# A count taken from the one-hots, a running sum moved behind the places, and three idle products in place of eight

## The chip, the cores and the metric

The kernel runs on one core of a Trainium2 chip. The metric is the device time of one execution in microseconds (us); lower is better. Engines are named as in the profile: PE is TensorE (PEld its weight loads), DVE is VectorE, ACT is ScalarE, POOL is GpSimd, SP is SyncE, whose queue issues the plain DMAs.

## The reference, cut to what matters

Two blocks act on 2048 rows of 128 numbers. The first has a causal attention with decay and, beside it, four layers of a mixture of 16 experts with one router each; a row goes to the one expert with the highest logit:

```python
def _unipool_layer(xt, router, W1, W2):
    probs = jax.nn.softmax(xt @ router, axis=-1)
    w, idx = jnp.max(probs, axis=-1), jnp.argmax(probs, axis=-1)
    def body(acc, params):
        w1, w2, i = params
        h = jax.nn.silu(xt @ w1) @ w2          # 128 -> 512 -> 128
        return acc + jnp.where(idx == i, w, 0.0)[:, None] * h, None
    ...
xt, _ = jax.lax.scan(step, xt, routers)        # L = 4 layers, E = 16 experts
```

The second block (a gated recurrence and a smaller mixture of experts) follows and is not touched.

## The kernel before

**Layers and tiles.** Each of the four layers works on rows sorted by expert, in 31 tiles of 128 rows (16 full tiles' worth of rows and 15 that padding may need). In `tile_mm` PE multiplies a tile by its expert's first matrix (L2258, 8 matmul records of a tile) and the tile before it by the second one (L2273, 8 records). The second product also gives the logits of the next layer's router. ACT scales and stores the result in `xrow` (L1722, `y_ev`).

**The next layer's order.** While a layer runs, its tiles' rows are placed for the next layer in six groups: tiles 0 to 7, 8 to 15, 16 to 19, 20 to 23, 24 to 27 and 28 to 30. For a group, DVE does four things. `choose` makes the one-hots `hot` (L1117 to L1125, `hot_ready`). `sum_hot` adds them up over the group's tiles and adds the sum so far (L1026, L1029, `hot_summed`). `weigh` makes the routing weight and copies the row's old place (L1138 to L1141). `rooms` and `place` turn counts and ranks into a row number for each row (L1002 to L1010, L1195 to L1202, `pos_ready`), and `carry_on` keeps what the next group needs (L1016 to L1020). Between `choose` and `rooms`, PE's `ranks` makes each row's rank within its expert and, at L2130, the count of each expert so far: one product of ones with `hot_sum[g]`. POOL scatters each tile's rows to memory by an indirect DMA (L734), one after the other, once the group's places are there.

**A helper.** `step(x)` makes DVE wait until x has ended; `mark(x)` only counts it. On DVE an instruction behind a `mark` may start before the marked one has ended.

**The end of a layer.** Groups 4 and 5 come behind the last tiles, and this stretch comes three times (ahead of layers 1, 2 and 3):

```python
choose(l, NGR - 2)
sum_hot(l, NGR - 2)
weigh(l, NGR - 2)
rooms(l, NGR - 2)
place(l, NGR - 2)
choose(l, NGR - 1)
weighted_scores(PHASE[l][0])
last_rooms(l)
```

PE does `ranks` of group 4 behind tile 30's place in the loop, then the last tiles' products, two products of attention scores (L2201), `last_ranks` (from L2141 on; it waits for `hot_ready`, `hot_summed` and `carried`), and a share of the attention (`retrieve` L2211, `scores` L2201), whose products alternate with DVE's weighting (L1217, L1219). Then it does eight products of the identity with itself into a corner of a bank that nobody reads (L2332; the profile records each as two matmuls):

```python
for n in range(WARM if l < L - 1 else 0):
    pe.matmul(PS[:, 1, 512 - P:512], ident[:, :], ident[:, :], start=True, stop=True)
```

**The start of the next layer.** SP waits until every scattered tile has landed (L610), then loads tile 0 and tile 1 (L587, one DMA each), the tags, and the other tiles in pairs (L596). PE waits for each of the first two tiles and transposes it (L2249); DVE copies three experts' matrices to a ring (L1259), then copies the two transposed tiles out (L1265); then PE begins the products of tile 0 (L2258).

Of the kernel before, what the change touches and what calls it, by code (L numbers as in the profile page):

```python
# [14 lines left out]
def build(nc, ins, out):  # L15
    x_in = ins["L0_attn_x"]
    B, S, D = x_in.shape
# [11 lines left out]
    NG = NT // G  # L29
# [9 lines left out]
    GROUPS = ((0, 8), (8, 16), (16, 20), (20, 24), (24, 28), (28, NS))  # L39
# [11 lines left out]
    WB = 4  # L51
    WARM = 8
    AHEAD = 2
# [99 lines left out]
    with ExitStack() as ctx:  # L153
# [788 lines left out]
        def _(dve):  # L942
            seq = [0]

            def step(ins_):
                seq[0] += 1
                ins_.then_inc(dve_seq, 1)
                dve.wait_ge(dve_seq, seq[0])
# [178 lines left out]
            def sum_hot(l, g):  # L1127

                tt = group_slots(g)
                dve.wait_ge(hot_ready, NG + l * NGR + g + 1)  # L1130
                dve.wait_ge(hot_summed, NG - 1 + l * (NGR - 1) + g)
                sum_so_far(g, hot[:, tt, :])

            def weigh(l, g):

                i, tt = NG + l * NGR + g, group_slots(g)
                dve.wait_ge(exp_done, i + 1)
                step(dve.tensor_scalar(ex[:, tt, :], ex[:, tt, :], -1.0, 1.0, ALU.mult, ALU.add))  # L1138
                step(dve.reciprocal(ex[:, tt, :], ex[:, tt, :]))
                mark(dve.tensor_reduce(xrow[:, tt, D + 1], ex[:, tt, :], AX_X, ALU.add))  # L1140
                step(dve.tensor_copy(xrow[:, tt, D], tags[:, GROUPS[g][0]:GROUPS[g][1], 0]))  # L1141

# [39 lines left out]
            def place(l, g):  # L1182
# [11 lines left out]
                else:  # L1194
# [7 lines left out]
                dve.tensor_tensor(pos[:, GROUPS[g][0]:GROUPS[g][1]], posf[:, tt], trash[:, GROUPS[g][0]:GROUPS[g][1]],  # L1202
                                  ALU.add).then_inc(pos_ready, 1)
                o = carry_on(g)
                if g == NGR - 2:
# [86 lines left out]
            for l in range(L):  # L1292
# [23 lines left out]
                if l < L - 1:  # L1316
                    choose(l, NGR - 2)
                    sum_hot(l, NGR - 2)
                    weigh(l, NGR - 2)
# [749 lines left out]
        def _(pe):  # L2069
# [39 lines left out]
            def ranks(l, g):  # L2109
# [4 lines left out]
                pe.wait_ge(hot_ready, i + 1)  # L2114
                if g < NGR - 1:
                    pe.wait_ge(hot_summed, NG - 1 + l * (NGR - 1) + g + 1)
                if g >= 2:
# [7 lines left out]
                for t in range(n - 1):  # L2125
                    later = o[:, (t + 1) * E:].rearrange("p (t e) -> p t e", e=E)
                    pe.matmul(later, ones_bf[:, :], hot[:, s0 + t:s0 + t + 1, :].to_broadcast([P, n - 1 - t, E]),
                              start=False, stop=(t == n - 2))
                if g < NGR - 1:
                    m = pe.matmul(o_count, ones_bf[:, :], hot_sum[:, g, :], start=True, stop=True)  # L2130
                m.then_inc(rank_mm, 1)

# [528 lines left out]
```

## Time and profile before

| | |
|---|---|
| median of 3 runs | 668.79 us (667.09 to 668.97) |
| the profiled execution, its own time | 668.92 us |
| its span, from the first to the last instruction | 667.1 us |
| mean granted clock of PE | 0.939 |
| PE busy | 578.5 us, 87% |
| DVE busy | 480.8 us, 72% |
| ACT busy | 433.2 us, 65% |
| POOL busy | 385.2 us, 58% |

The profile records one execution. Busy times are shares of the span; 1.8 us of the profiled execution's time lie outside the span. The granted clock is that of PE as a share of 2.4 GHz. In the views below a number before a name is the start in us from the span's start.

### The profile page before, as it was taken

How to read it: one execution, taken by the hardware profiler on the slowest of the kernel's cores; microseconds unless marked ns; L12 is line 12 of the kernel's file. 1: busy time of each engine (PE TensorE's matmuls, PEld its weight loads, DVE VectorE, ACT ScalarE, POOL GpSimd, SP SyncE). 2: the span in 40 equal slices, each digit the busy share in tenths (PEclk: the TensorE clock that was granted, in tenths of full speed). 3: DMA queues.
4: the chain of work that ended last, by engine and by line, in shares of the span. 5: the costliest groups of instructions: out<-in, count | busy, mean ns of one | idle time of the engine just before them, and what ended most of it. 6: DMA issues, size and time to landing. Idle time of an engine off the chain costs nothing.

```text
span 667.1 us, 14440 instructions
## 1 busy us (share of the span) xinstructions
PE 578.5 (87%) x4659; PEld 492.3 (74%) x4659; DVE 480.8 (72%) x1407; ACT 433.2 (65%) x1016; POOL 385.2 (58%) x433
## 2 busy tenths in 40 slices
PE   1969899999999999979999598977867877798896
PEld 1759899959997799959999346955645664576785
DVE  7543456874588556875321789889999999997946
ACT  4374366754677356735677578978877887887533
POOL 7372005740357104752546311786999999998974
PEclk9979899999999999979999888869888788989999
DMA  7953264226521373115331200000000000000002
GB/s 250 344 183 39 59 175 78 60 52 143 101 59 50 56 169 73 53 51 66 73 63 44 64 1 1 2 1 1 1 1 0 0 1 2 0 1 1 2 2 64
DMA packets 109690, 39.86 MB, mean 60 GB/s; under 512 B 86098, under 2 KB 103538, under 8 KB 109490
## 3 DMA queue, kind: packets, MB, share of 16 engines
q1 hardware_dynamic: 105138, 29.64, 20.1%
q0 software_dynamic: 4480, 9.30, 4.1%
q8 instruction: 40, 0.66, 0.4%
q14 instruction: 32, 0.26, 0.1%
HBM read 20.32 MB, written 18.59 MB: 58 GB/s over the span
## 4 chain that ended last, share of the span: by engine, by line
PE 56%; DVE 29%; ACT 7%; POOL 5%; issue 3%; DVEq 0%; POOLq 0%
PE PS L2273 17%; PE PS L2258 16%; PE PS L2211 3%; ACT W1s L1897 2%; PE PS L2177 2%; DVE W1s L1521 2%; DVE W1s L1490 2%; DVE W2s L1376 2%; PE PS L2440 2%; DVE PS L1492 2%; DVE PS L1494 2%; DVE PS L1514 2%; DVE PS L1496 2%; PE PS L2201 2%; PE PS L2456 2%
## 5 line engine op out<-in xcount | busy, mean ns | idle before, releaser
L734 POOL DMA_INDIRECT sorted_x<-xrow,pos x93 | 90.5, 973 | 148.6 <-ACT xrow L1722 77.8
L2273 PE MATMUL PS<-W2s,hbuf 128*128 x992 | 140.1, 285 | 0.0
L2258 PE MATMUL PS<-hbuf,swt 128*128 128x128 f32 x992 | 132.6, 278 | 2.9 <-DVE hbuf L1265 2.9
L2273 PEld LDWEIGHTS PS<-W2s,hbuf 128*128 128x128 f32 x992 | 127.7, 192 | 0.4
L2258 PEld LDWEIGHTS PS<-hbuf,swt 128*128 128x128 f32 x992 | 121.7, 193 | 3.7 <-DVE swt L1259 2.0
L1714 ACT ACTIVATE hbuf<-PS 128x512 f32<-128x512 f32 x124 | 73.1, 590 | 51.9 <-PE PS L2258 49.5
L1722 ACT ACTIVATE xrow<-PS,tags 128x144 f32<-128x144 f32 (+1 forms) x124 | 46.8, 377 | 42.3 <-PE PS L2273 40.3
L1897 ACT ACTIVATE W1s<-W1s,ab 128x128 f32<-128x128 f32 x168 | 51.3, 391 | 16.4 <-DVE W1s L1524 16.3
L2440 PE MATMUL PS<-ewT,xT 128*128 128x512 f32 x64 | 38.6, 735 | 21.5 <-ACT W2s L1948 21.4
L850 POOL TENSOR_TENSOR W1s<-W1s,kT 128x1024 f32<-128x1024 f32 x22 | 52.3, 2383 | 7.0 <-DVE W1s L1524 5.8
L1259 DVE COPY swt<-W1s 128x512 f32 x64 | 27.1, 427 | 38.5 <-PE PS L2258 34.5
L739 POOL DMA_INDIRECT results<-xrow,pos x31 | 31.1, 1004 | 37.8 <-ACT xrow L1722 25.8
L1268 DVE STREAM_TRANSPOSE hbuf<-hbuf 128x128 f32<-128x128 f32 x116 | 33.3, 300 | 18.0 <-DMA hbuf<-sorted_x 16.8
L2456 PEld LDWEIGHTS PS<-W2s,ident 128*128 128x128 f32 x256 | 35.4, 215 | 11.8 <-issue 11.8
L1765 ACT ACTIVATE swt<-W1s 128x512 f32 x60 | 37.8, 631 | 3.2 <-issue 1.1
L2492 PE MATMUL PS<-ident,W1s 128*128 128x128 f32 x256 | 34.7, 280 | 5.6 <-POOL W1s L850 5.6
L1948 ACT ACTIVATE W2s<-PS,selbuf 128x128 f32<-128x128 f32 x128 | 35.1, 368 | 4.3 <-issue 4.0
L2440 PEld LDWEIGHTS PS<-ewT,xT 128*128 128x128 f32 x64 | 13.0, 226 | 33.0 <-ACT W2s L1948 23.1
L2456 PE MATMUL PS<-W2s,ident 128*128 128x128 f32 x256 | 35.2, 297 | 1.7 <-DVE xres L1438 1.7
L2492 PEld LDWEIGHTS PS<-ident,W1s 128*128 128x128 f32 x256 | 29.5, 144 | 7.2 <-POOL W1s L850 6.5
L1897 ACT ACTIVATE W1s<-xrow,ab 128x128 f32<-128x128 f32 x88 | 26.9, 397 | 8.5 <-DVE xrow L1524 8.5
L1219 DVE SCALAR_TENSOR_TENSOR wdec<-PS,wdec 128x512 f32<-128x512 f32 (+3 forms) x24 | 13.4, 556 | 22.1 <-PE PS L2201 21.4
(420 smaller groups left out, 1356.2 us busy)
## 6 DMA issues: line engine op xcount, KB each, us to landing
hbuf<-sorted_x SPq DMA_DIRECT2D x224, 32.0 KB
sorted_x<-slotbuf SPq DMA_DIRECT2D x9, 520.0 KB, 3.7
W2s<-in_L_ffn_W_dram SPq DMA_DIRECT2D x16, 256.0 KB, 5.0
W1s<-in_L_ffn_W_dram SPq DMA_DIRECT2D x1, 4096.0 KB, 16.8
sorted_x<-slotbuf SPq DMA_DIRECT2D x1, 2015.0 KB, 7.9
sorted_x<-xrow,pos POOLq DMA_INDIRECT x109, 2.4
sorted_x<-slotbuf SPq DMA_DIRECT2D x3, 455.0 KB, 2.9
xres<-in_L_attn_x_dram SPq DMA_DIRECT2D x4, 256.0 KB, 3.6
```

What stands on the lines that cost most here:

```text
L734: pool.indirect_dma_start(xs_dram[l + 1][:, :], bass.IndirectOffsetOnAxis(ap=pos[:, t:t + 1], axis=0), xrow[:, t % NR, 0:XW], None).then_i ...
L850: pool.tensor_tensor(qX[t % QR], X[(t + 1) % NX], Qc[:, t, :, :].unsqueeze(1).to_broadcast([P, 2 * HD, HP, HD]), ALU.mult).then_inc(r_read ...
L1714: act.activation(hTs[:, (c - 1) % 2, :], PS[:, 2 + (c - 1) % 2, :], ACT.Silu).then_inc(h_act, 1)
L1722: act.activation(xrow[:, t % NR, 0:w], PS[:, 4 + c % 2, 0:w], ACT.Copy, scale=tags[:, t, 1:2]).then_inc(y_ev, 1)
L1765: act.activation(w1st[:, c % WB, :], W1s[:, bass.ds(w, FF)], ACT.Copy).then_inc(w1_act, 1)
L1897: o = act.activation(aX[:, :, h, :], X[t % NX][:, :, h, :], ACT.Copy, scale=ab[:, t, h:h + 1])
L1948: o = act.activation(scaled[:, t % 2, e, :], PS[:, 4 + e // 4, e % 4 * D:(e % 4 + 1) * D], ACT.Copy, scale=sel[:, t, e:e + 1])
L2258: m = pe.matmul(PS[:, 2 + n, f * P:(f + 1) * P], w1st[:, (c - 1) % WB, f * P:(f + 1) * P], xring[:, (c - 1) % R, :], start=True, stop=True)
L2273: m = pe.matmul(PS[:, 4 + n, 0:w], hTs[:, n, f * P:(f + 1) * P], W2s[:, f * YW:f * YW + (E - 1) * NF + w][:, bass.ds(w2, w)], start=(f == ...
L2440: m = pe.matmul(PS[:, 4 + n, :], xT[:, t * P:(t + 1) * P], ewT[:, n * 512:(n + 1) * 512], start=True, stop=True)
L2456: pe.matmul(o, ident[:, :], scaled[:, t % 2, e, :], start=(e == 0), stop=False)
L2492: m = pe.matmul(o, qXw[t % QR][:, i, :], ident[:, :], is_transpose=True, start=(i == 0), stop=(i == HD - 1))
```

## The change

Three edits. (1) For group 4 the count no longer comes from `hot_sum[4]`: PE multiplies ones by `hot_sum[3]` and by each of the four tiles' one-hots and adds the five in the bank, so `ranks` of group 4 waits for the one-hots and for the sum of group 3; `sum_hot` of group 4 moves from ahead of `weigh` into `place`, behind the write of the places and ahead of `carry_on`. (2) In `weigh`, for all five groups that use it, the copy at L1141 is marked and not waited for. (3) `WARM` goes from 8 to 3.

```diff
-    WARM = 8
+    WARM = 3
...
                 mark(dve.tensor_reduce(xrow[:, tt, D + 1], ex[:, tt, :], AX_X, ALU.add))
-                step(dve.tensor_copy(xrow[:, tt, D], tags[:, GROUPS[g][0]:GROUPS[g][1], 0]))
+                mark(dve.tensor_copy(xrow[:, tt, D], tags[:, GROUPS[g][0]:GROUPS[g][1], 0]))
...
                                   ALU.add).then_inc(pos_ready, 1)
+                if g == NGR - 2:
+                    sum_hot(l, g)
                 o = carry_on(g)
...
                     choose(l, NGR - 2)
-                    sum_hot(l, NGR - 2)
                     weigh(l, NGR - 2)
...
-                if g < NGR - 1:
-                    pe.wait_ge(hot_summed, NG - 1 + l * (NGR - 1) + g + 1)
+                pe.wait_ge(hot_summed, NG - 1 + l * (NGR - 1) + (g + 1 if g < NGR - 2 else g))
...
-                if g < NGR - 1:
+                if g < NGR - 2:
                     m = pe.matmul(o_count, ones_bf[:, :], hot_sum[:, g, :], start=True, stop=True)
+                else:
+                    pe.matmul(o_count, ones_bf[:, :], hot_sum[:, g - 1, :], start=True, stop=False)
+                    for t in range(n):
+                        m = pe.matmul(o_count, ones_bf[:, :], hot[:, s0 + t, :], start=False, stop=(t == n - 1))
                 m.then_inc(rank_mm, 1)
```

## Rows read from the trace of the kernel before

**Rows 1.** Busy us (x instructions) of PE, PEld, DVE, ACT, POOL in layer 1, PEclk, DMA

```profile
150.00:200.00 50.00, 50.00 (x444) 49.81 (x444) 31.24 (x123) 31.96 (x66) 14.86 (x16) 1.00 0.48 100
```

**Rows 2.** Chain that ended last, group 4 ahead of layer 1: start, us, what

```profile
131.03 0.23 DVE hot L1125
...
131.29 0.27 DVE hot_sum L1026
...
131.59 0.17 DVE hot_sum L1029
131.75 0.35 DVE ex L1138
...
132.85 0.17 DVE xrow L1141
...
133.04 0.19 DVE room L1002
...
135.46 0.16 DVE pos L1202
135.63 0.10 DVE shift L1016
```

**Rows 3.** The same chain, from the attention's products to the transposes of layer 1

```profile
145.28 1.98 PE PS L2211 x4
147.26 1.78 PE PS L2332 x16
149.05 0.12 PE PS L2249
```

**Rows 4.** Timeline around group 4's ranks and group 5's choice ahead of layer 1

```profile
130.32 0.26 ACT L1729 ACTIVATE ex<-selbuf 128x64 f32<-128x64 f32 x1 [0.55 <-DVE selbuf L1118]
...
131.85 0.19 PE L2121 MATMUL PS<-hot,ltri 128*128 128x64 bf16 x1 [0.62 <-DVE hot L1125]
...
131.91 0.22 PE L2127 MATMUL PS<-hot,ones_bf 128*128 128x48 bf16 x3
...
135.20 0.38 ACT L1722 ACTIVATE xrow<-PS,tags 128x144 f32<-128x144 f32 x1 [0.65 <-PE PS L2273]
...
136.04 0.20 DVE L1117 TENSOR_REDUCE mx<-xrow 128x3 f32<-128x48 f32 x1
```

**Rows 5.** Timeline of scatters, group 5's places, SP's first loads and PE's transposes

```profile
135.90 0.97 POOL L734 DMA_INDIRECT sorted_x<-xrow,pos  x1 [1.26 <-DVE pos L1202]
...
140.23 0.16 DVE L1180 TENSOR_TENSOR pos<-posf,trash 128x3 int32<-128x3 f32 x1
...
140.98 0.97 POOL L734 DMA_INDIRECT sorted_x<-xrow,pos  x1 [0.31 <-issue]
...
145.96 0.82 SPq L587 DMA_DIRECT2D hbuf<-sorted_x  x2
...
148.78 0.25 PEld L2249 LDWEIGHTS PS<-ident,hbuf 128*128 128x128 f32 x2
```

**Rows 6.** L587, the loads of tiles 0 and 1: ahead of layer 1, then one of layer 2

```profile
DMA to landing us min/median/max: 1.7/1.8/1.9
...
L587 SPq DMA_DIRECT2D hbuf<-sorted_x x1: 426/426/426, 222.8 to 222.8; - x1
...
DMA to landing us min/median/max: 2.1/2.1/2.1
```

**Rows 7.** Timeline ahead of layer 2 (first row) and of layer 3

```profile
225.04 0.25 PEld L2249 LDWEIGHTS PS<-ident,hbuf 128*128 128x128 f32 x2
...
298.52 0.81 SPq L587 DMA_DIRECT2D hbuf<-sorted_x  x2
...
302.00 1.36 DVE L1259 COPY swt<-W1s 128x512 f32 x3 [0.19 <-issue]
...
304.29 0.49 DVE L1265 COPY hbuf<-PS 128x128 f32<-128x128 f32 x2 [0.93 <-PE PS L2249]
```

**Rows 8.** Single microseconds ahead of layer 3 (columns as in group 1; PEclk third from last)

```profile
289.00:290.00 1.00, 0.00 (x0) 0.00 (x0) 0.86 (x6) 0.99 (x5) 0.69 (x2) 1.00 0.12 29
...
292.00:293.00 1.00, 0.33 (x3) 0.13 (x1) 0.88 (x5) 0.61 (x1) 0.73 (x1) 0.61 0.20 67
...
299.00:300.00 1.00, 1.00 (x4) 0.46 (x4) 0.64 (x2) 0.00 (x0) 0.00 (x0) 0.98 0.28 67
```

## The prediction

> **What bounds the kernel now.** I read a window inside a layer first, to see whether PE has slack there. It has none: it is busy for 50.00 of 50 us inside layer 1 [rows 1], at full clock, and layers 2 and 3 have the same loop, so a layer that starts earlier ends earlier by as much. Then I read the chain that ended last through the stretch ahead of layer 1. It goes first through DVE, one instruction after the other with about 0.02 us between them, from the choice of group 4 to the places [rows 2]; from the attention's products on it goes through PE, on which the idle products stand between the last L2211 and the transposes, 1.78 us for 16 records [rows 3]. The stretches ahead of layers 2 and 3 have the same order. Last I read the timeline for what runs beside this chain and could take its place: PE's ranks and ACT's last result [rows 4], POOL's scatters and the loads that wait for them [rows 5, 6], the stage copies of DVE [rows 7], and PE's clock [rows 8].
>
> **The sum behind the places (and the count from the one-hots).** Removed ahead of `weigh`: L1026 waits for L1125 and starts 0.26 us after it (131.29 against 131.03), L1029 follows at 131.59, and L1138 runs in the chain from 131.75, its start being about 0.08 us after L1029's, 131.67. So L1138 starts 0.64 us after L1125 [rows 2]. With the sum gone it follows a 64-column instruction that it needn't wait for; independent neighbours start some 0.15 us apart for that size (L1029 to L1138 was 0.08 with 16 columns, so 0.08 to 0.22 are the bounds, L1125's whole 0.23 being the upper one). I take 0.15: the places of group 4 come 0.49 us earlier. The cover is ACT's L1729, done at 130.58, long before L1138 needs it [rows 4].
> Put back: behind the places, L1026 starts where L1016 did, 0.17 us after L1202's start, less the overlap, then 0.30 us to L1029, and 0.08 us to L1016: 0.38 us ahead of `carry_on` (bounds 0.3 and 0.5, by whether the neighbours overlap). Net on DVE: 0.49 - 0.38 = 0.11 us gained.
> Added on PE: five count products in place of one. L2127's three such small products take 0.22 us together and follow each other at about 0.03 us [rows 4], so four more cost 0.12 us, at most 0.3 by their full lengths. But `ranks` now starts at `hot`'s end (131.26) and not behind the sum (L2121 began at 131.85, having waited 0.62 us), so it ends some 0.4 us earlier than before. DVE needs the count at 133.04 less 0.6; PE is done by 132.0. The last tile's result on ACT moves with PE: its end was 135.58, with 0.46 us to spare before L1117 at 136.04 [rows 4], so DVE's gain is not cut there.
> Queued behind the moved sum: `carry_on`, `choose` of group 5, and through `carried` PE's `last_ranks`. The sum stands ahead of `carried`, and `last_ranks` waits for the one-hots of group 5, later than both. No new wait ends last.
>
> **The mark.** L1141 starts at 132.85 and L1002 at 133.04, 0.19 us [rows 2]; marked, a 16-column neighbour starts about 0.08 us behind. Gained: 0.11 us (bounds 0 and 0.17) in group 4. The twelve instances in groups 0 to 3 lie beside a PE that never waits [rows 1]: nothing.
> So DVE reaches everything behind `carry_on` 0.22 us earlier, and the places of group 4 are 0.6 us earlier.
>
> **What POOL does with it.** The first scatter of group 4 starts at 135.90 behind the places, having waited 1.26 us, so POOL is free in time; it starts 0.6 us earlier. The fifth, the first of group 5, started at 140.98 [rows 5], so they follow each other at 5.08/4 = 1.27 us. Now it would be ready at 140.38, but its places (L1180) end at 140.39 - 0.22 = 140.17 [rows 5], and 0.28 us passes from places to scatter (135.46 + 0.16 to 135.90), so 140.45: 0.53 us earlier. The last scatter and SP's first load, at 145.96, move by the same 0.53 us. Ahead of layer 2 the rows repeat. Ahead of layer 3 the loads don't matter: issued from 298.52 on, with the 2 us of such loads they are there by 301, and PE's transposes only fed L1265 at 304.29 [rows 6, 7].
>
> **Three idle products in place of eight.** Ten of 16 records go: 10/16 of 1.78 us [rows 3] = 1.11 us. With DVE's 0.22 us PE would be ready for tile 0's transposes 1.33 us earlier. What is late next:
> Ahead of layer 1 it is tile 1's load. Its issue is the second of the two that start at 145.96 and last 0.82 us together, so at 146.36, and it lands after 1.9 us [rows 5, 6]: 148.26, less 0.53 us is 147.73. The second transpose's weights went in at about 148.90 (the second of two in 0.25 us from 148.78) [rows 5]; PE would be there at 147.57, so the load decides by 0.2 us, and with a few hundredths from landing to PE the gain is 1.1 us.
> Ahead of layer 2 tile 1's load starts at 222.8 and takes 2.1 us [rows 6]: 224.9, less 0.54 is 224.4 against PE's second transpose at about 225.15 [rows 7]: gain 0.75 us.
> Ahead of layer 3 the loads came early; there DVE's three stage copies end at 303.36 [rows 7], less 0.22 is 303.14, and then L1265 can follow; it started at 304.29, having waited 0.93 us for PE [rows 7]. Gain 1.1 us.
>
> **Sum.** 1.1 + 0.75 + 1.1 = 2.95 us. The profiled execution took 668.92 us, 0.13 above the median of the runs: 665.97, about 665.9 against the median. If no load and no copy stood in the way it would be 3 x 1.33 = 4.0 us (664.9); if the sum and the mark gave nothing at all, the loads would let 0.55, 0.25 and 0.9 through, 1.7 us (667.1).
>
> **The rivals.**
> *The loads take the gain (chance 0.13).* If DVE's moved sum delays group 5 as much as it helps group 4, or the landing is slower by a few tenths, tile 1's load ends last ahead of layers 1 and 2. For it: 1.7 to 2.1 us for the same kind of load [rows 6]. Against it: POOL's wait of 1.26 us on the places shows that they are what its queue starts from. Time: 668.9 - 1.9 = 667.0, within 0.3%.
> *The clock falls once more (0.12).* PE's granted clock fell to half (1.2 GHz) in 292 to 293 us, behind a microsecond without any product, and was back at 2.4 GHz in 299 to 300, some 6.8 us later [rows 8]. In dense tiles 6.8 us at half speed cost 3.4; between layers, where PE and DVE alternate, I take 2.7 of that. The change starts `ranks` earlier and so leaves PE longer without work ahead of `last_ranks`, and it takes away 1.1 us of products at the end. One such fall more, ahead of layer 1 or 2, gives 668.7 to 669.4. Against it: ahead of layer 1 the clock held with PE's stretches as they were, and PE's wait ahead of `last_ranks` grows there only by 0.4 - 0.2 = 0.2 us; dense work follows the idle products within 1 us.
> The Trainium skill, "TensorE: Matmul & The Clock Gate", section "What's actually happening", says that the throttled clock is the default and that activity releases it. By that rule the five products taken away speak against this change; the trace agrees in that its fall comes behind an idle PE.
> *The clock falls in two of the three stretches (0.05), the one that ends on the other side.* Its place is the start of layers 1 and 2, in dense tiles at 3.4 us each: -2.95 + 6.8 = +3.9, 672.8; it decides when both stretches lose the clock, since one fall alone only takes the gain back.
> *The fall ahead of layer 3 goes away or shifts out of the chain (0.09).* It came behind PE's idling, which the change moves by tenths of a microsecond, and no row says how near it was to not falling: -2.95 - 2.7, 663.3.
> *The forecast (0.61).* Its own range is 664.9 to 667.0.
>
> **How the numbers follow.** 0.3% is 2.0 us here, about what a measurement of this kernel can tell from no change; the three runs span 1.9. Faster (under 666.8): the forecast but its upper edge 0.57, and the vanished fall 0.09: 0.66. Same: the forecast's edge 0.04, the loads 0.13, most of the single fall 0.09: 0.26. Slower: the rest of the single fall 0.03 and the double one 0.05: 0.08. The range goes from 664.2, with the bounds of the forecast and a part of the vanished fall, to 668.8, which takes in the loads and about half of the single fall.
>
> **What would show it.** In the profile of the changed kernel L2332 should have 18 matmuls in place of 48; L1026 and L1029 of group 4 should stand behind L1202; the first scatter of group 4 should start about 4.3 us after that group's L1125 (135.90 - 131.03 = 4.87 before); PE's weight load for the second transpose should show a wait for the load of tile 1 ahead of layers 1 and 2, of some tenths, and DVE's L1265 no wait ahead of layer 3. The prediction is wrong if PE waits there for over 0.7 us (the loads), if the clock is below 1 in 137 to 152 or 213 to 228 us (the clock), or if L1117 of group 5 waits for ACT.

## The result and the profile after

The changed kernel took 663.37 us in the median of 7 runs (660.62 to 665.49), the kernel before 668.67 (666.57 to 668.97) beside it on the same chip: a ratio of 0.9929, interval 0.9901 to 0.9956. By the medians 5.3 us were gained, by the means (668.10 and 663.34) 4.8, where 2.95 were forecast. The direction was right and the time lies below the forecast range.

The profiled execution took 661.22 us (span 659.5, mean clock 0.935), 7.7 less than that of before. Not all of this is the change's. The first product of layer 0 came at 71.02 instead of 72.78, and PE's clock didn't fall in the layer's first microseconds as it did at 73.8 before. Over the profiles of this study it comes between 70.6 and 73.2; the changed kernel alone had it at 71.02, 72.90, 70.58 and 73.08 in its four profiles, so the edits don't set it. These 1.8 us, 1.4 us by which layer 0 was shorter in this profile, and the 4.4 us below make up the 7.7. What the change does stands in the three stretches between group 4's first instruction (L1117) and the first product of the next layer. I measure them all from that L1117, so that what came earlier drops out:

| us from group 4's L1117, ahead of layer 1 / 2 / 3 | before | after |
|---|---|---|
| places of group 4 (L1202) | 5.65 / 5.65 / 5.65 | 4.79 / 4.79 / 4.80 |
| L1117 of group 5 | 6.23 / 6.22 / 6.23 | 5.77 / 5.76 / 5.77 |
| last places (L1180) | 10.42 / 10.41 / 10.66 | 9.89 / 9.88 / 10.12 |
| first load issued | 16.15 / 16.33 / 16.16 | 16.15 / 15.45 / 15.56 |
| weights of the first idle product | 16.86 / 16.84 / 19.72 | 16.31 / 16.31 / 18.90 |
| first product of the next layer | 19.82 / 19.80 / 22.37 | 18.87 / 18.22 / 20.52 |

The three gains are 0.95, 1.58 and 1.85, together 4.38 us of the 4.8 to 5.3. Between a first product and the next group 4 the two profiles agree within 0.01 us in layers 1 and 2 (56.47 and 56.46 us). Forecast were 1.1, 0.75 and 1.1.

**DVE and PE in group 4.** In the changed kernel the lines behind L1202 have moved by two, those of PE by four, so L1715, L1723 and L1267 are L1714, L1722 and L1265 of before, L2215, L2253, L2262 and L2336 are L2211, L2249, L2258 and L2332. The timeline of the changed kernel ahead of layer 1, which answers to [rows 2, 4, 5]:

```profile
127.80 0.97 POOL L734 DMA_INDIRECT sorted_x<-xrow,pos  x1 [0.30 <-issue]
127.85 0.22 DVE L1125 TENSOR_TENSOR hot<-rt,first 128x64 bf16<-128x64 f32 x1
127.99 0.19 DVE L1138 TENSOR_SCALAR ex<-ex 128x64 f32<-128x64 f32 x1
128.12 0.10 PEld L2121 LDWEIGHTS PS<-hot,ltri 128*128 128x128 bf16 x1 [0.30 <-DVE hot L1125]
...
128.30 0.24 PE L2134 MATMUL PS<-hot,ones_bf 128*128 128x16 bf16 x4
...
129.00 0.17 DVE L1002 TENSOR_SCALAR room<-PS 128x16 f32<-128x16 f32 x1
...
131.41 0.16 DVE L1202 TENSOR_TENSOR pos<-posf,trash 128x4 int32<-128x4 f32 x1
131.49 0.26 DVE L1026 TENSOR_REDUCE hot_sum<-hot 128x16 bf16<-128x64 bf16 x1
...
131.85 0.97 POOL L734 DMA_INDIRECT sorted_x<-xrow,pos  x1 [0.53 <-DVE pos L1202]
...
132.39 0.20 DVE L1117 TENSOR_REDUCE mx<-xrow 128x3 f32<-128x48 f32 x1
```

The sum stands behind the places, and POOL starts 4.00 us after L1125 (forecast 4.3, before 4.87). L1138 begins 0.14 us after L1125 (forecast 0.15), but it takes 0.19 us where it took 0.42 before. The four new products take 0.24 us together and are done 0.46 us before L1002 needs them.

**What ends last ahead of layers 1 and 2.** The timeline ahead of layer 1:

```profile
142.77 0.82 SPq L587 DMA_DIRECT2D hbuf<-sorted_x  x2
...
144.72 0.77 PE L2253 MATMUL PS<-ident,hbuf 128*128 128x128 f32 x2 [0.52 <-DMA hbuf<-sorted_x]
145.06 0.29 DVE L1267 COPY hbuf<-PS 128x128 f32<-128x128 f32 x1 [1.56 <-PE PS L2253]
...
145.16 0.14 PEld L2253 LDWEIGHTS PS<-ident,hbuf 128*128 128x128 f32 x1 [0.33 <-DMA hbuf<-sorted_x]
...
145.49 2.02 PE L2262 MATMUL PS<-hbuf,swt 128*128 128x128 f32 x16
145.52 0.29 DVE L1267 COPY hbuf<-PS 128x128 f32<-128x128 f32 x1 [0.17 <-PE PS L2253]
```

and ahead of layer 2:

```profile
217.41 0.81 SPq L587 DMA_DIRECT2D hbuf<-sorted_x  x2
...
219.38 0.14 PEld L2253 LDWEIGHTS PS<-ident,hbuf 128*128 128x128 f32 x1
...
219.75 0.29 DVE L1267 COPY hbuf<-PS 128x128 f32<-128x128 f32 x1 [0.92 <-PE PS L2253]
...
219.83 0.14 PEld L2253 LDWEIGHTS PS<-ident,hbuf 128*128 128x128 f32 x1 [0.31 <-DMA hbuf<-sorted_x]
220.15 0.97 PEld L2262 LDWEIGHTS PS<-hbuf,swt 128*128 128x128 f32 x8 [0.19 <-issue]
220.18 1.02 PE L2262 MATMUL PS<-hbuf,swt 128*128 128x128 f32 x7
220.19 0.29 DVE L1267 COPY hbuf<-PS 128x128 f32<-128x128 f32 x1 [0.16 <-PE PS L2253]
```

PE waits 0.33 and 0.31 us for the load of tile 1, as forecast, but this is not the wait that ends last. Tile 0's products need tile 0's own copy, the first L1267, and through it the first transpose and the load of tile 0. PE waits 0.52 us for that load ahead of layer 1; ahead of layer 2 no wait stands in the row, but the first weights go in 0.10 us after the load has landed (the table under tile1_late_c has the landings), as ahead of layer 1. The copy of tile 0 then runs while PE waits for tile 1, and the products start 0.43 us behind the copy's start (145.06 to 145.49, 219.75 to 220.18). They start 0.33 and 0.35 us behind the second transpose's weights, where 0.17 us is enough (tile1_late_c below), and PE's weight loads sat idle between the two, 0.19 us ahead of layer 2. So tile 1's load had 0.17 us to spare ahead of layer 1 and 0.19 ahead of layer 2. Before, both copies came behind both transposes. The timeline of the kernel before ahead of layer 2, whose transposes' weights are the first row of [rows 7]:

```profile
225.46 0.49 DVE L1265 COPY hbuf<-PS 128x128 f32<-128x128 f32 x2 [1.98 <-PE PS L2249]
...
225.90 0.79 PE L2258 MATMUL PS<-hbuf,swt 128*128 128x128 f32 x5 [0.37 <-DVE hbuf L1265]
```

There the first product came 0.75 us after the second weights (225.15), and 0.44 us after the start of tile 0's copy.

Ahead of layer 1 the loads are issued no earlier after group 4's start than before, though the last places are 0.53 us earlier. The chain that ended last shows why: its first row is the landing of the last scatter, 3.14 us, which took 2.3 to 2.5 in the other five stretches of the two profiles. (Its last row is tile 1's load, issued at 143.17, since the view steps from the product to the transpose before it on PE and not to the copy that the product waited for.)

```profile
139.49 3.14 DMA sorted_x<-xrow,pos
...
143.17 1.95 DMA hbuf<-sorted_x
```

**Ahead of layer 3.** The timeline there:

```profile
292.21 0.81 SPq L587 DMA_DIRECT2D hbuf<-sorted_x  x2
...
295.47 1.36 DVE L1261 COPY swt<-W1s 128x512 f32 x3 [0.18 <-issue]
...
295.66 0.83 PE L2336 MATMUL PS<-ident 128*128 128x128 f32 x6
...
296.33 0.38 PE L2253 MATMUL PS<-ident,hbuf 128*128 128x128 f32 x2
296.74 0.48 DVE L1267 COPY hbuf<-PS 128x128 f32<-128x128 f32 x2
```

L1267 waits for nothing but DVE's own stage copies, as forecast. The six records of L2336 take the place of sixteen in 1.95 us. The windows by single microseconds, columns as in [rows 1], answer to [rows 8]:

```profile
287.00:288.00 1.00, 0.35 (x1) 0.35 (x2) 0.93 (x4) 0.00 (x0) 0.79 (x1) 0.72 0.20 67
...
289.00:290.00 1.00, 1.00 (x2) 0.00 (x1) 0.31 (x2) 0.41 (x1) 0.69 (x2) 0.50 0.01 0
290.00:291.00 1.00, 1.00 (x4) 0.12 (x3) 0.00 (x0) 0.00 (x0) 0.73 (x1) 0.57 0.21 67
291.00:292.00 1.00, 1.00 (x5) 0.49 (x4) 0.86 (x4) 0.40 (x1) 0.00 (x0) 1.00 0.20 67
```

The clock's fall to 1.2 GHz is still there, but it lasts 3.4 us (from 287.4) where it lasted 6.8.

### The profile page after: what moved, and what is told of

Its sections match the earlier page's. It is cut to its first block, busy times and chain, and to the rows that moved or that the text cites. A ratio compares the mean times of both kernels' runs of the same rounds, so it can differ in the third digit from the quotient of the medians.

```text
span 659.5 us, 14389 instructions
## 1 busy us (share of the span) xinstructions
PE 570.4 (86%) x4641; PEld 483.2 (73%) x4641; DVE 478.9 (73%) x1407; ACT 433.4 (66%) x1016; POOL 386.4 (59%) x433
## 3 DMA queue, kind: packets, MB, share of 16 engines
HBM read 20.32 MB, written 18.59 MB: 59 GB/s over the span
## 4 chain that ended last, share of the span: by engine, by line
PE 51%; DVE 33%; ACT 7%; POOL 4%; issue 3%; DMA 1%; DVEq 0%; SPq 0%; POOLq 0%; ACTq 0%
PE PS L2277 17%; PE PS L2262 16%; DVE W2s L1377 3%; PE PS L2181 2%; DVE W1s L1522 2%; DVE W1s L1491 2%; ACT W1s L1898 2%; DVE PS L1493 2%; DVE PS L1515 2%; DVE PS L1495 2%; DVE PS L1497 2%; DVE W1s L1525 2%; DVE W1s L1513 2%; PE PS L2605 1%; PE PS L2172 1%
## 5 line engine op out<-in xcount | busy, mean ns | idle before, releaser
L2262 PE MATMUL PS<-hbuf,swt 128*128 128x128 f32 x992 | 131.8, 276 | 2.2 <-DVE hbuf L1267 2.2
L2262 PEld LDWEIGHTS PS<-hbuf,swt 128*128 128x128 f32 x992 | 121.0, 192 | 3.0 <-DVE swt L1261 2.6
L1715 ACT ACTIVATE hbuf<-PS 128x512 f32<-128x512 f32 x124 | 73.2, 590 | 47.4 <-PE PS L2262 45.5
L1723 ACT ACTIVATE xrow<-PS,tags 128x144 f32<-128x144 f32 (+1 forms) x124 | 46.9, 378 | 41.6 <-PE PS L2277 38.8
```

The costliest lines, as they stand in the source:

```text
L1715: act.activation(hTs[:, (c - 1) % 2, :], PS[:, 2 + (c - 1) % 2, :], ACT.Silu).then_inc(h_act, 1)
L1723: act.activation(xrow[:, t % NR, 0:w], PS[:, 4 + c % 2, 0:w], ACT.Copy, scale=tags[:, t, 1:2]).then_inc(y_ev, 1)
L2262: m = pe.matmul(PS[:, 2 + n, f * P:(f + 1) * P], w1st[:, (c - 1) % WB, f * P:(f + 1) * P], xring[:, (c - 1) % R, :], start=True, stop=True)
```

## The experiments

Two questions: what made DVE's part 0.46 us where 0.22 were forecast, and what of the rest comes from the idle products, the loads and the clock. Theory P says that L1138 was slow because of where it fell beside a scatter of POOL.

### The three edits apart

warm3_alone is the kernel before with 3 idle products; mark_alone has the marked copy alone; sum_and_mark is the changed kernel with 8 idle products; sum_alone is that, with the copy waited for.

```diff
-    WARM = 8                                                       # warm3_alone
+    WARM = 3
...
-                step(dve.tensor_copy(xrow[:, tt, D], tags[...]))   # mark_alone
+                mark(dve.tensor_copy(xrow[:, tt, D], tags[...]))
...
-    WARM = 3                                                       # sum_and_mark, sum_alone
+    WARM = 8
...
-                mark(dve.tensor_copy(xrow[:, tt, D], tags[...]))   # sum_alone
+                step(dve.tensor_copy(xrow[:, tt, D], tags[...]))
```

> The kernel before with three idle products in place of eight and nothing else. I measure the three stretches between layers from L1117 of group 4 to the first product of tile 0 of the next layer (before: 19.82, 19.80 and 22.37 us; with the whole change: 18.87, 18.22 and 20.52). Theory A (the gain of the change arises in these stretches, and what a stretch gives is set by the load of tile 1 or the stage copies once the idle products are gone): PE is ready 1.12 us earlier in each; tile 1's load stays where it was, so the stretches come to about 18.87, 19.17 and 21.45, together 2.5 us less than before. Theory B (my forecast's step: the wait for tile 1's load delays everything behind it by as much, since both copies to the ring follow both transposes): 19.25, 19.55 and 21.45, together 1.7 us less. Rival C (the gain of the change came from PE's clock or from work ahead of the layers, not from these stretches): the stretches shrink by no more than 1 us together and the time stays within 1 us of before.

> Only the sum behind the places and the count from the one-hots; the copy in weigh is waited for as before and there are eight idle products. Theory A: group 4's places come 0.73 us earlier after its L1117 (4.9 us in place of 5.65), 0.49 of it from the sum and 0.24 from L1138, which should take 0.19 us in place of 0.43 since it no longer meets a certain part of POOL's scatter; group 5's L1117 comes 0.35 us earlier. Each stretch shrinks by about 0.35 to 0.45 us, 1.2 together. Rival (L1138's duration has nothing to do with where it starts): it stays at 0.43 us and the stretches shrink by 0.1 to 0.15 us each.

> Only the copy in weigh is marked and not waited for. Both theories: L1141 to L1002 goes from 0.19 to 0.08 us, group 4's places and all behind them come 0.11 us earlier, and each stretch shrinks by 0.1 us, 0.3 together. L1138 still starts where it did against POOL's scatter and still takes 0.42 us.

> The whole change but for the idle products: eight as before. Theory A: DVE's part of each stretch is that of the changed kernel (group 5's L1117 5.77 us after group 4's, against 6.23), PE is the last to be ready for the transposes by over a microsecond, no load is waited for, so each stretch shrinks by about 0.5 us, 1.5 together; together with three idle products alone (2.5) that makes up 4.0 of the 4.38 us that the whole change took off. Rival C: the time is as that of before and the whole change's gain is not the sum of its parts.

Measured, with the kernel before at 667.83 us (25 runs) beside them:

| | median us | ratio, interval | L1138 us | places | group 5's L1117 | first product |
|---|---|---|---|---|---|---|
| before | 667.83 | | 0.42 | 5.65 | 6.23 | 19.82 / 19.80 / 22.37 |
| mark_alone | 669.21, one run | | 0.29 | 5.40 | 5.98 | 19.56 / 19.53 / 22.50 |
| sum_alone | 667.96 | 0.9998, 0.997 to 1.0026 | 0.19 | 4.92 | 5.89 | 19.40 / 19.41 / 21.50 |
| sum_and_mark | 666.21 | 0.9968, 0.9947 to 0.999 | 0.19 | 4.79 | 5.77 | 19.27 / 19.27 / 21.59 |
| warm3_alone | 665.05 | 0.9947, 0.9926 to 0.9967 | 0.42 | 5.66 | 6.24 | 18.83 / 18.86 / 20.80 |
| after | | | 0.19 | 4.79 | 5.77 | 18.87 / 18.22 / 20.52 |

(us from group 4's L1117, ahead of layer 1 where one number stands.) The idle products alone are worth 3.50 us by the three stretches and 3.5 by the ratio. Ahead of layers 1 and 2 they gave 0.99 and 0.94, where theory B (my forecast's step, a fixed distance behind tile 1) said 0.57 and 0.25; that step is refuted. Sum and mark together 1.86 by the stretches and 2.1 by the ratio. sum_alone's stretches are 1.68 shorter, which its interval just holds. The two parts don't add up (5.36 against 4.38): the shorter fall of the clock is in both, and ahead of layer 1 the slow landing took some 0.6 us back (1.58 ahead of layer 2, 0.95 there). (One of sum_and_mark's ten executions took 679.96 us; the ratio leaves it out.) Marking the copy gives 0.13 us behind the moved sum, near the 0.11 forecast, but 0.25 alone: there L1138 began 0.67 us behind a scatter's start and not 0.58, and took 0.29 us and not 0.42. The mark in the groups before, by which POOL's scatters start some 0.1 us earlier, is the likely reason.

### A later start for L1138 and nothing else

one_more_dve is the kernel before with one needless instruction on DVE ahead of `weigh` of group 4.

```diff
                     sum_hot(l, NGR - 2)
+                    step(dve.tensor_tensor(last_room[:, :], one_e[:, :], one_e[:, :], ALU.add))
                     weigh(l, NGR - 2)
```

> The kernel before with one more DVE instruction of 16 columns, waited for, between the sum and weigh of group 4 (0.19 us; its result is not used). In the kernel before L1138 starts 0.58 us after the start of a POOL scatter and takes 0.42 us; with only the copy marked it started 0.67 us after and took 0.29; in the changed kernel it starts 0.18 us after and takes 0.19. Theory P (a scatter holds something that L1138 needs from about 0.6 to 0.8 us after its start): L1138 now starts 0.76 us after the scatter and takes 0.19 us, so the places of group 4 come after 5.6 us as before, though an instruction of 0.19 us was added. Rival (L1138 is slow because it follows the small sum): it follows a small instruction here too, takes 0.42 again, and the places come at 5.84 us.

Its timeline ahead of layer 1:

```profile
131.41 1.01 POOL L734 DMA_INDIRECT sorted_x<-xrow,pos  x1 [0.30 <-issue]
...
132.00 0.17 DVE L1319 TENSOR_TENSOR last_room<-one_e 128x16 f32<-128x16 f32 x1
132.20 0.22 DVE L1138 TENSOR_SCALAR ex<-ex 128x64 f32<-128x64 f32 x1
132.45 0.55 DVE L1139 RECIPROCAL ex<-ex 128x64 f32<-128x64 f32 x1
```

The instruction took 0.21 us of the chain and L1138 gave 0.20 back; the places came at 5.66, 5.65 and 5.66, as in the kernel before, and the first products at 19.81, 19.81 and 22.48 (before 19.82, 19.80 and 22.37). The one execution took 669.56 us and the kernel before beside it 666.24, which single executions can't tell apart. So work was added and the places got no later: L1138's 0.42 us isn't its own length, and the rival, that it is slow behind a small instruction, is out. The timelines of the kernel before, with each DVE instruction beside the scatter that it started behind:

```profile
131.09 1.01 POOL L734 DMA_INDIRECT sorted_x<-xrow,pos  x1 [0.30 <-issue]
...
131.67 0.42 DVE L1138 TENSOR_SCALAR ex<-ex 128x64 f32<-128x64 f32 x1
...
132.40 0.97 POOL L734 DMA_INDIRECT sorted_x<-xrow,pos  x1 [0.30 <-issue]
...
132.85 0.16 DVE L1141 COPY xrow<-tags 128x4 f32<-128x4 f32 x1
...
291.00 0.96 POOL L734 DMA_INDIRECT sorted_x<-xrow,pos  x1 [0.30 <-issue]
291.57 0.36 DVE L1146 COPY xrow<-tags 128x3 f32<-128x3 f32 x1
```

and of mark_alone:

```profile
131.24 0.97 POOL L734 DMA_INDIRECT sorted_x<-xrow,pos  x1 [0.30 <-issue]
131.91 0.29 DVE L1138 TENSOR_SCALAR ex<-ex 128x64 f32<-128x64 f32 x1
```

Started 0.58 us behind a scatter's start L1138 took 0.42 us, at 0.67 it took 0.29, at 0.79 0.22, and at 0.19 (the changed kernel) 0.19. The copy L1146 took 0.36 at 0.57 us, and 0.17 at 0.45 ahead of layer 1. So each ended 0.93 to 1.0 us after the scatter's start if it began in a narrow part of it. Over the eight undisturbed profiles (these four, sum_alone, sum_and_mark, warm3_alone, tile1_late_c) L1138 of this size began 72 times within 1.4 us of a scatter's start: nine times at 0.57 to 0.68 us, taking 0.28 to 0.43; three times at 0.76 to 0.79, taking 0.22; and 60 times elsewhere, taking 0.14 to 0.20. This is theory P. Which of the two is held up isn't fixed by the offset: a larger copy of the kernel before that began 0.57 us behind a scatter kept its usual 0.43 us, and the scatter took 1.12 instead of 0.97.

```profile
98.89 1.12 POOL L734 DMA_INDIRECT sorted_x<-xrow,pos  x1 [40.92 <-ACT xrow L1722]
...
99.46 0.43 DVE L1259 COPY swt<-W1s 128x512 f32 x1 [0.21 <-PE PS L2258]
```

The Trainium skill, "SBUF — State Buffer", section "Who interferes with whom", says that DVE's copy and tensor_scalar can enter a mode in which they use the port pair that DVE shares with GpSimd, and that whoever issues first has it for the whole instruction. The trace agrees in who meets whom: behind the middle of a scatter only those two kinds were slowed. It differs in the extent: L1138 and the small copies ran at full speed in the first 0.45 us of a scatter.

### What ends last behind the idle products

tile1_late puts the tags' load between tile 0's and tile 1's; one_load loads both tiles with one DMA, which both transposes wait for; no_idle is the changed kernel without idle products; after_again is the changed kernel itself.

```diff
-                for c in range(ROWS_FIRST):                        # tile1_late
-                    load_rows(c)
+                load_rows(0)
                 load_tags(0)
+                load_rows(1)
...
-    WARM = 3                                                       # no_idle
+    WARM = 0
...
+                sp.dma_start(xring[:, 0:ROWS_FIRST, :],            # one_load, in place of two
+                             xs_tiles[l][:, 0:ROWS_FIRST, 0:D]).then_inc(ld_first[0], 16)
```

> The changed kernel as it is, once more. In the profiles so far the three stretches account for 4.4 us of the gain, about 0.55 of it from a clock fall ahead of layer 3 that lasted 3.4 us in place of 6.8; the rest of the 7.7 us between the two profiled executions lay ahead of layer 0 (1.8 us) and in a clock fall in layer 0's first tiles (1.4). Theory A: the stretches repeat within 0.1 us (18.9, 18.2 to 18.9, 20.5 to 21.1), the first product of layer 0 starts at 72.6 to 73.0 us as in the other profiles and not at 71.0, and the time is 3.5 to 4.5 us below that of before over many runs. Rival D (the change also shortens the work ahead of layer 0): it starts at 71.0 again.

> The changed kernel with no idle product at all. Theory A (tile 1's load or the stage copies set the end of each stretch, and PE already waits 0.3 us for the load with three): the stretches ahead of layers 1 and 2 don't shrink, the one ahead of layer 3 by 0.1 us at most, the same time within 0.5 us. The clock: if the idle products hold it, it falls between 137 and 152 or 213 and 228 us, and the time rises by 2.7 us or more for each fall; if dense work starts soon enough, it stays at full speed.

> The changed kernel with tiles 0 and 1 of each layer loaded by one DMA in place of two; PE waits for it ahead of both transposes. Theory A: tile 1 lands about 0.4 us earlier, tile 0 perhaps 0.3 later; PE no longer waits between the two transposes, but tile 0's copy then starts later. Stretches ahead of layers 1 and 2 change by -0.3 to +0.2 us each, that of layer 3 not at all.

> The changed kernel with the tags' load issued between tile 0's and tile 1's, so tile 1's load is issued 0.45 us later. Theory A (tile 1's load ends last ahead of layers 1 and 2, and not ahead of layer 3): those two stretches grow by 0.45 us each, to about 19.3 and 18.7, PE's wait between the two transposes grows from 0.3 to 0.75 us, and the stretch ahead of layer 3 stays at 20.5. Rival E (PE itself or DVE's copies end last there): all three stay.

These four ran on another chip, on which the kernel before took 701.95 us. after_again took 699.97 (ratio 0.9973, 0.9946 to 1.0000), no_idle 699.84 (0.9971, 0.9936 to 1.0006), one_load 701.10 (0.9994, 0.9966 to 1.0022), tile1_late 700.96 in one run. In the changed kernel's profile the 30 us and more lie in waits of ACT and DVE inside the layers (last section); of the kernel before no trace from that chip is kept. They move DVE against PE in the stretches too: the count of group 4 is taken some 5.5 us after L1117 instead of 2.4. So the length of a stretch can't be compared, and the four say only that after_again, no_idle and one_load aren't told apart there. The same four once more:

> The changed kernel as it is, once more, since the chip of the last four runs took 702 us for the kernel before as well and stood still several times inside the layers. On a chip without that, Theory A: the stretches ahead of layers 1, 2 and 3 repeat (18.9, 18.2 to 18.9, 20.5 to 21.1 us), the first product of layer 0 starts at 72.6 to 73.0 us as in the other profiles and not at 71.0, and the time is 3.5 to 4.5 us below that of before. Rival D: layer 0 starts at 71.0 again.

> The changed kernel with no idle product at all. Theory A: the loads or the stage copies set the end of each stretch, so those ahead of layers 1 and 2 shrink by 0.1 us at most and that of layer 3 by 0.1 us; the same time within 0.5 us. If idle products hold the clock, it falls between 137 and 152 or 213 and 228 us, and the time rises by 2.7 us or more for each fall.

> The changed kernel with tiles 0 and 1 of each layer loaded by one DMA in place of two; PE waits for it ahead of both transposes. Theory A: PE no longer waits between the two transposes, but starts them later; the stretches ahead of layers 1 and 2 change by -0.3 to +0.2 us each, that of layer 3 not at all.

> The changed kernel with the tags' load issued between tile 0's and tile 1's, so tile 1's load is issued 0.45 us later. Theory A (tile 1's load ends last ahead of layers 1 and 2, and not ahead of layer 3): those two stretches grow by 0.45 us each, PE's wait between the two transposes grows from 0.3 to 0.75 us, and the stretch ahead of layer 3 stays. Rival E (PE itself or DVE's copies end last there): all three stay.

A third chip showed the same waits (before 701.99): after_b 700.12 (0.9996, 0.9962 to 1.0031), no_idle_b 700.01 (0.997, 0.9935 to 1.0004), one_load_b 703.52 (1.0043, 1.0007 to 1.0079), tile1_late_b 701.64. The one finding is that one DMA for both tiles doesn't help there: in one_load_b it was slower than the kernel before.

> The changed kernel with the tags' load between tile 0's and tile 1's, once more, for a profile on a chip without the standstills. Theory A: the stretches ahead of layers 1 and 2 grow by 0.45 us each (tile 1's load is issued 0.45 us later), PE's wait between the two transposes grows from 0.3 to 0.75 us, and the stretch ahead of layer 3 stays. Rival E: all three stay.

This one, beside one_more_dve, ran undisturbed (before 666.24, tile1_late_c 665.45, one run each). Its timeline ahead of layer 1:

```profile
147.20 0.30 PE L2253 MATMUL PS<-ident,hbuf 128*128 128x128 f32 x1
...
147.53 0.29 DVE L1267 COPY hbuf<-PS 128x128 f32<-128x128 f32 x1 [1.19 <-PE PS L2253]
...
148.51 0.33 PE L2253 MATMUL PS<-ident,hbuf 128*128 128x128 f32 x1 [1.02 <-DMA hbuf<-sorted_x]
...
148.68 1.51 PE L2262 MATMUL PS<-hbuf,swt 128*128 128x128 f32 x12
148.88 0.29 DVE L1267 COPY hbuf<-PS 128x128 f32<-128x128 f32 x1 [1.05 <-PE PS L2253]
```

Tile 1's load was issued 0.86 us behind tile 0's, 0.47 later than in the changed kernel, and also took 0.4 to 0.6 us longer to land. The traces of four kernels give, in us from group 4's L1117, ahead of layer 1 / 2:

| | before | warm3_alone | after | tile1_late_c |
|---|---|---|---|---|
| tile 0's load landed | 17.90 / 18.07 | 17.91 / 17.94 | 17.96 / 17.32 | 17.61 / 17.62 |
| first transpose's weights | 18.96 / 18.94 | 18.02 / 18.05 | 18.06 / 17.42 | 17.71 / 17.72 |
| start of tile 0's copy | 19.38 / 19.36 | 18.39 / 18.42 | 18.43 / 17.79 | 18.08 / 18.09 |
| tile 1's load landed | 18.48 / 18.79 | 18.54 / 18.42 | 18.49 / 17.83 | 19.02 / 19.31 |
| second transpose's weights | 19.07 / 19.05 | 18.59 / 18.46 | 18.53 / 17.87 | 19.06 / 19.35 |
| first product | 19.82 / 19.80 | 18.83 / 18.86 | 18.87 / 18.22 | 19.22 / 19.52 |

In the first three kernels the first product follows the start of tile 0's copy by 0.43 or 0.44 us, while its distance from the second transpose's weights goes from 0.75 down to 0.24. Only in tile1_late_c is tile 1 the last to be ready: there the product follows the second weights by 0.16 or 0.17 us, and the start of tile 0's copy by 1.14 and 1.43. A layer thus starts at the later of two times: tile 0's copy plus 0.44 us, and the second transpose's weights plus 0.17. This gives all 60 starts of layers 1 to 3 in the 20 profiles, the disturbed ones included, within 0.01 us.

So a tile 1 that comes 0.5 us or more later does delay layers 1 and 2, as theory A expected (19.22 and 19.52 instead of 18.87 and 18.22), but this doesn't show that its load ends last in the changed kernel. There tile 0's load does: the first transpose's weights go in 0.10 us behind its landing, and tile 1 has 0.17 and 0.19 us to spare. Ahead of layer 3 neither load matters; the first product came at 20.42 instead of 20.52.

The last group also looks for something beyond the change. turn_first has no idle product, and in every layer DVE copies the two transposed tiles out behind its second stage copy and not behind its third:

```diff
-    {0: (), 1: (), 2: (0, 1), 3: (2, 3, 4)}
+    {0: (), 1: (0, 1), 2: (), 3: (2, 3, 4)}
```

> The changed kernel once more, beside the two below. Theory A on a chip without standstills: stretches of 18.9, 18.2 to 18.9 and 20.4 to 20.6 us, layer 0's first product at 72.4 to 73.0 us in most runs, and a time 3.5 to 4.5 us below that of before.

> The changed kernel without any idle product. Theory A: the loads of tiles 0 and 1 end last ahead of layers 1 and 2, the stage copies ahead of layer 3: the stretches change by 0.1 us at most, the time by less than 0.5 us. If the idle products hold the clock, it falls between 137 and 152 or 213 and 228 us, and the time rises by 2.7 us or more for each fall.

> No idle product, and DVE copies the two transposed tiles out behind its second stage copy and not behind its third. Theory A: ahead of layer 3, where the third stage copy (0.43 us) stands between the transposes and the copies out, the stretch shrinks by about 0.4 us to 20.1; ahead of layers 1 and 2, where a load comes last, it stays. Together 0.4 us less than without idle products: too little for the times to tell, so the stretches decide.

> The changed kernel with tiles 0 and 1 loaded by one DMA. Theory A: no wait between the transposes ahead of layers 1 and 2, the first transpose later by 0.2 to 0.5 us, the stretches changed by -0.3 to +0.2 us; the one ahead of layer 3 as it is.

Another chip, and the waits again (before 701.57): after_c 700.97 (0.9973, 0.9941 to 1.0005), no_idle_c 700.29 (0.9994, 0.9965 to 1.0022), turn_first 699.71 (0.9977, 0.9944 to 1.0011), one_load_c 698.65 in one run. One execution of after_c took 2999.67 us, for a reason that no trace shows; the ratio leaves it out. No difference is beyond the intervals. In the four profiles without idle products (no_idle, no_idle_b, no_idle_c and turn_first) the clock fell at other places of the layers, but no fall began between 5 us ahead of the first product of layer 1 or 2 and 30 us behind it.

## Why the forecast was too small

**The idle products** were costed about rightly. Ahead of layer 3, from the weights of the first idle product to the first product of tile 0 it was 2.65 us before and 1.62 after: 1.03, forecast 1.11.

**DVE's own terms** held too: L1138 0.14 us behind L1125, 0.40 us for the sum behind the places (0.38), 0.13 for the mark (0.11), four products of PE unseen. What was wrong is "the places of group 4 come 0.49 us earlier": sum_alone measured 0.73. The step took every instruction that stays to keep its length. L1138's 0.42 us held 0.23 of waiting beside a scatter, and the move took it out of that spot. So 0.86 at the places instead of 0.60, and 0.46 behind `carry_on` instead of 0.22. This is a mis-sized term, and a row for it was there: the chain's 0.35 for L1138 stands beside 0.23 for L1125 of 64 columns [rows 2].

**POOL and the loads.** Group 5's first scatter came 0.84 us earlier (10.33 against 11.17 us after group 4's L1117; forecast 0.53), since both the queue and the last places had moved. Ahead of layer 2 the loads came 0.88 earlier, ahead of layer 3 0.60, and ahead of layer 1 not at all: there 3.14 us for the last scatter's landing ate it. sum_and_mark has the same late loads ahead of layer 1 (16.23, against 15.43 ahead of layer 2), sum_alone hasn't (15.43). The last scatter's landing took 3.14 and 3.21 us in those two cases, and 2.8 to 3.0 ahead of layer 1 in mark_alone and tile1_late_c, so it doesn't go by the edits. What makes a landing slow stays open.

**The step that failed** is "Ahead of layer 1 it is tile 1's load ... so the load decides" and its like ahead of layer 2, "gain 0.75 us". The sum compared two times for PE's second transpose and kept the 0.75 us from there to tile 0's first product. But the product doesn't wait for that transpose's result. It waits for tile 0's copy, 0.44 us behind the copy's start in every case, and the copy needs the first transpose only. What ended last was tile 0's load. The 0.75 us are simply what was left when both transposes stood in a row; when PE waits for tile 1 in between, the copy runs under that wait, and 0.33 and 0.35 us are left. tile1_late_c marks the limit, 0.17.

Read by the path that holds, the gain is the first transpose's: 0.90 us ahead of layer 1 and 1.52 ahead of layer 2. Another 0.05 comes since the copy starts 0.37 us behind a transpose that stands alone and 0.42 behind the first of two in a row. That gives 0.95 and 1.57. With the forecast's own terms (PE ready 1.33 us earlier, loads 0.53 or 0.54 earlier) this path would have given, as an estimate from the table above, about 1.38 and 1.36 and with layer 3's 1.1 together 3.84 us, 665.1. The forecast's 1.1 ahead of layer 1 was near by luck: it had the wrong load and the wrong distance, and the loads, which it moved by 0.53 us, didn't move at all.

**Layer 3 and the clock.** 1.85 is 1.03 of the idle products and 0.82 ahead of them, for which DVE's 0.22 were forecast. warm3_alone, with DVE as before, has 0.54 of this (the first idle product's weights at 19.18 instead of 19.72), and its fall of the clock is 3.4 us long like that of the changed kernel. Counted from group 4's L1117, the clock was down from 9.9 to 16.7 us in the kernel before [rows 8], and from 11.9 to 15.3 in warm3_alone. mark_alone and one_more_dve kept the 6.8 us and gained nothing there. So about half a microsecond comes from a shorter fall, with DVE's earlier work for the rest. The rival "the fall goes away" named a real cause, but priced it too high: it took 2.7 us for 6.8 us of fall, and half of the fall was worth about 0.5. Its 663.3 us is near the measured 663.37 by luck. Why a slow microsecond costs so little there was not tested; DVE's weighting beside it is the likely reason. sum_alone and sum_and_mark have the shorter fall with all eight idle products. What sorts the eight undisturbed profiles is where the fall began: at 9.86, 10.08 and 10.41 us after group 4's L1117 it lasted 6.8 us (before, one_more_dve, mark_alone), at 10.56 to 11.88 it lasted 3.4 (sum_alone, tile1_late_c, after, sum_and_mark, warm3_alone). And in all seven of them that have a fall in layer 0, the one ahead of layer 3 began 215.0 us after that one had ended, whatever the edits. So a kernel that gains time ahead of layers 1 and 2 comes to this stretch earlier and meets the fall later in it, which would explain why warm3_alone has the shorter one. That is argued from the order of eight profiles; no run moved the stretch alone.

**The other rivals.** The loads did take a part, but tile 0's and not tile 1's: PE waited 0.52 us for it ahead of layer 1. No clock fall came ahead of layer 1 or 2 in any undisturbed run, with three idle products or eight. The Trainium skill, "TensorE: Matmul & The Clock Gate", section "What's actually happening", says that activity releases the throttle, which spoke against taking products away; these runs show five fewer at no cost. Whether the last three do anything for the time stays open, since no_idle ran on disturbed chips alone, where it made no difference.

**The sum.** With the terms as measured: ahead of layer 1 0.90 + 0.05, ahead of layer 2 1.52 + 0.05 (1.58 before rounding), ahead of layer 3 0.82 + 1.03, together 4.38. Of the 1.4 us over the forecast, 0.9 is the path through tile 0 in place of tile 1 (3.84 against 2.95), 0.75 is layer 3, of which about 0.5 is the clock, and 0.2 is that the loads ahead of layer 2 came 0.88 us earlier in place of 0.54; the late landing ahead of layer 1 took 0.4 of it back.

## What to carry to other kernels

Before you take an instruction's time from a profile as its length, compare it with neighbours of its kind and size: one that is twice as long is waiting for something, and moving it by 0.1 us can be worth more than what you removed. When you cost "what is late next", start from what the next work itself waits for and go back from there: the load that lands last can have time to spare. A distance between two instructions is fixed only if the second waits for the first. Measure each stretch from a common first instruction, since two profiled executions can differ by 3 us ahead of anything that was changed.

## What the runs showed of the hardware

**A scatter of POOL holds up some of DVE for a fifth of a microsecond.** DVE's tensor_scalar from and to SBUF, and its copy, took 0.35 to 0.43 us instead of 0.17 to 0.19 if they began 0.57 to 0.59 us after the start of an indirect DMA's instruction of 0.97 us, and their own length at 0.19 and 0.45 us. The scatters that L1138 met at 0.58 and 0.79 us ahead of layer 1 took 1.01 instead of 0.97, the one met at 0.67 kept its 0.97. A copy of 128x512 elements at 0.57 us kept its 0.43, and the scatter took 1.12. A smaller effect is seen on several kinds: DVE instructions that began within about 0.05 us ahead of a scatter's start took 0.05 to 0.07 us longer, as L1141 with 0.22 instead of 0.16, and also tensor_tensor (0.29 instead of 0.22).

**On three of the chips the kernels stood still inside the layers.** There the kernel before took about 702 us instead of 668 and the changed one 700 to 701 instead of 663. The instructions kept their usual lengths, ACT's L1715 for one with a mean of 591 ns (590 in the undisturbed profile). In the changed kernel's profiles from there (none of the kernel before is kept) ACT and DVE waited again and again for signals of PE that had been due microseconds before. The timeline of after_again in layer 1:

```profile
225.56 0.24 PE L2134 MATMUL PS<-hot,ones_bf 128*128 128x16 bf16 x4
...
229.42 0.17 DVE L1002 TENSOR_SCALAR room<-PS 128x16 f32<-128x16 f32 x1 [3.07 <-remote]
```

and its costliest groups (the last field is what ended the idle time before them):

```profile
L1715 ACT ACTIVATE hbuf<-PS 128x512 f32<-128x512 f32 x124 | 73.3, 591 | 63.3 <-PE PS L2262 44.9 <-remote 14.1 <-issue 4.2
...
L1723 ACT ACTIVATE xrow<-PS,tags 128x144 f32<-128x144 f32 (+1 forms) x124 | 46.7, 376 | 64.0 <-PE PS L2277 47.5 <-remote 10.5 <-issue 5.4
```

PE's count products ended at 225.8, and L1002, which waits for them alone, began at 229.42; "remote" means that no event of this profile released it. In after_again the distance between the first products of layers 0 and 1 was 88.2 us instead of 74.5, between those of layers 1 and 2 85.5 instead of 74.7. No profile from the other chips has any wait put down to "remote". What causes them stays open.
